# A front without queries and a lag of two slices in a gated mixture-of-experts block on one core

## The reference

```
kv   = ctx @ Wk.T + bk
sim  = ((LN(x) @ kv) @ kv.T) / 16              # 256 x 256 per batch
attn = softmax((sim - mean) * rsqrt(var + 1e-6) * gamma + beta)
x1   = x + tanh(g0) * attn
h    = LN(x1)
score = sigmoid(h @ Wg.T)                      # 16 experts in 4 groups
# with a bias: best two groups by their top two, in them the top 4 experts;
# weights = the scores of those four, normalised, times 2.5
out  = x1 + tanh(g1) * (shared(h) + sum_e weight_e * down_e(silu(gate_e h) * up_e h))
```

## Time and profile before

| | us |
|---|---|
| median of 3 runs | 194.6 (194.2 to 194.71) |
| profiled execution, its time | 194.61 |
| its span in the profile | 192.8 |
| PE busy | 183.1 (95%) |
| DVE busy | 147.1 (76%) |
| ACT busy | 81.2 (42%) |
| POOL busy | 83.0 (43%) |

### The profile page before, as it was taken

The page is one execution under the profiler, slowest core; times in us unless marked ns, Lnnn a source line. Parts: engine busy times, 40 slices in busy tenths (PEclk is TensorE's granted clock), DMA queues, the critical chain, the costliest instruction groups (busy, mean ns, idle before and its releaser), DMA issues.

```text
span 192.8 us, 3265 instructions
## 1 busy us (share of the span) xinstructions
PE 183.1 (95%) x1003; PEld 151.9 (79%) x1003; DVE 147.1 (76%) x332; ACT 81.2 (42%) x160; POOL 83.0 (43%) x101
## 2 busy tenths in 40 slices
PE   6999799969899999999999989999999999999993
PEld 5665457858788888888788868888888888888882
DVE  1759988989899699998469999885666665566664
ACT  2449725523248833435457333434334343433220
POOL 2352162822841755553345543454444555444410
PEclk9999999999999999999999999999999999999999
DMA  5967200002785555541221000312211221221403
GB/s 145 344 212 217 76 0 0 0 0 57 235 205 183 150 141 163 161 139 58 54 54 54 0 3 9 109 57 74 80 60 54 54 54 60 74 78 60 143 20 112
DMA packets 10297, 18.08 MB, mean 94 GB/s; under 512 B 1773, under 2 KB 3821, under 8 KB 10286
## 3 DMA queue, kind: packets, MB, share of 16 engines
q1 hardware_dynamic: 9504, 17.11, 29.4%
q10 hardware_dynamic: 782, 0.83, 1.8%
HBM read 16.82 MB, written 1.11 MB: 93 GB/s over the span
## 4 chain that ended last, share of the span: by engine, by line
PE 67%; DVE 20%; DMA 6%; issue 2%; POOL 1%; ACT 1%; DVEq 0%; SPq 0%; POOLq 0%
PE bank L782 41%; PE bank L834 8%; PE bank L826 7%; PE bank L828 7%; DMA xs<-x_in 3%; DVE act_hi L553 2%; DVE bank L556 2%; DVE act_lo L561 2%; DMA w_row<-weight_rows 2%; DVE stats L458 1%; POOL rstd L278 1%; PE bank L712 1%; DMA weight_rows<-w_blk 1%; DVE beats L597 1%; PE bank L752 1%
## 5 line engine op out<-in xcount | busy, mean ns | idle before, releaser
L284 POOL TENSOR_TENSOR w_lo<-w_raw,w_hi 128x256 fp32r<-128x256 f32 (+1 forms) x72 | 72.4, 1024 | 76.7 <-ACT w_hi L327 75.6
L327 ACT CAST w_hi<-w_raw 128x256 fp32r<-128x256 f32 (+2 forms) x72 | 36.5, 513 | 56.4 <-PE bank L834 30.6
L782 PE MATMUL bank<-hT_hi,w_hi 128*128 128x512 f32 x142 | 56.5, 398 | 0.0
L782 PE MATMUL bank<-hT_lo,w_hi 128*128 128x512 f32 x142 | 56.0, 395 | 0.0
L782 PE MATMUL bank<-hT_hi,w_lo 128*128 128x512 f32 x142 | 44.7, 396 | 0.0
L535 DVE TENSOR_TENSOR weighted<-bank,w_row 128x512 f32<-128x512 f32 x30 | 20.7, 691 | 25.6 <-ACT bank L386 24.5
L826 PE MATMUL bank<-w_hi,act_hi 128*128 128x256 f32 x144 | 36.0, 283 | 1.8 <-DVE act_hi L553 1.8
L828 PE MATMUL bank<-w_lo,act_hi 128*128 128x256 f32 x144 | 35.8, 281 | 0.0
L782 PEld LDWEIGHTS bank<-hT_hi,w_lo 128*128 128x128 f32 x142 | 26.7, 188 | 6.3
L782 PEld LDWEIGHTS bank<-hT_hi,w_hi 128*128 128x128 f32 x142 | 26.8, 189 | 5.1
L826 PEld LDWEIGHTS bank<-w_hi,act_hi 128*128 128x128 f32 x144 | 27.2, 189 | 4.3 <-issue 2.8
(11 more groups left out here) (100 smaller groups left out, 133.2 us busy)
## 6 DMA issues: line engine op xcount, KB each, us to landing
w_row<-weight_rows SPq DMA_DIRECT2D x31, 256.0 KB, 3.2
w_raw<-w_in SPq DMA_DIRECT2D x18, 384.0 KB, 3.9
xs<-x_in SPq DMA_DIRECT2D x4, 256.0 KB, 5.9
out<-x SPq DMA_DIRECT2D x2, 256.0 KB, 3.5
cw<-ctxw_in ACTq DMA_DIRECT2D x1, 276.2 KB
vec<-vecs_in ACTq DMA_DIRECT2D x1, 265.0 KB, 5.6
out<-x SPq DMA_DIRECT2D x2, 128.0 KB, 1.8
out<-x ACTq DMA_DIRECT2D x2, 128.0 KB, 1.8
```

Of the source, the lines that this page charges most:

```text
L284: nc.gpsimd.tensor_tensor(w_lo[:, par, cols], w_raw[:, bass.ds(n, 1), cols].rearrange("p o c -> p (o c)"), w_hi[:, par, cols].bitcast(F32) ...
L327: nc.scalar.copy(w_hi[:, par, cols], w_raw[:, bass.ds(n, 1), cols].rearrange("p o c -> p (o c)"))\
L782: last = nc.tensor.matmul(dst, w[:, par, w0 + c * P:w0 + (c + 1) * P], m, start=i == 0, stop=i == len(parts) - 1, skip_group_check=True)
```

## The change

1. Front without queries. The host passes x transposed too (xT), and the context with a row of ones, as columns (cT) and as rows. PE makes `square` = Wk' Wk from the augmented weights, u = square times the centred context (`projected`), r = context rows times xT (`gathered`), and sim = r u. Centring the context (`centre_context`, DVE for batches 0 and 1, ACT for 2 and 3) takes the mean out of sim. x isn't normalised any more; a term `row_eps` of x's variance goes into the variance of sim instead.
2. Logits of batches 0 and 1. POOL multiplies u with gamma (`u_times_gamma`), PE makes a second product from it (`similarity_gamma`), ACT scales its rows by the inverse root (`scale_rows`), and one DVE operation adds -beta and takes the minimum (L547, `tensor_tensor_reduce`); exp has the scale -1. Batches 2 and 3 keep scale, add and maximum on DVE.
3. The table of exp is loaded early by an activation on two columns; contexts lead the queues of SP and ACT.
4. Lag of two: in step k PE does down of k-2. act_hi, act_lo and the down weights (now d_hi, d_lo) have three buffers. gate(k) still waits for `act_done` of k-2.
5. Gate and up of slices 0 and 1 for batch 0 run on PE before the transposes of batch 1 (`early_gate`, `early_up`), with pieces of batches 2 and 3 between; `route(0)` stands inside step 0 and `route_back(0)` inside step 1.
6. DVE's routing of half 0 stands in one piece after step 1. The late multiplications of slices 2 and 3 by the weight row (`late_parts`) move to step 3 and write to SBUF.
7. All loops are unrolled; the load of a weight row waits for `actlo_done` where it waited for `act_done`.

The core of the diff:

```diff
+            def u_times_gamma(b):
+                pool.wait_ge(u_ready, b + 1)
+                nc.gpsimd.tensor_tensor(uT_gamma[:, b, :], uT[:, b, :], gamma_key[:], ALU.mult)\
+                  .then_inc(u_gamma_ready, 1)
...
+            def scale_rows(b):
+
+                act.wait_ge(rstd_ready, b + 1)
+                for i, t in enumerate(tiles(b)):
+                    act.wait_ge(scaled_done, 2 * b + i + 1)
+                    nc.scalar.activation(scaled[:, t, :], scaled_ps[b][i], ACT.Identity,
+                                         scale=rstd[:, 1, t:t + 1]).then_inc(scaled_read, 1)
...
+            table_change = {7: lambda: (softmax_exp(2), softmax_exp(3)), 16: lambda: logit_exp(1)}
+
+            u_copy(0)
+            r_copy(0)
+            offset_copy(1)
+            r_copy(1)
+            u_copy(1)
+            scale_rows(0)
+            softmax_exp(0)
+            high_gu(0)
...
             hidden_high(1)
+            offset_copy(3)
+            u_copy(3)
             logitT_copy(0)
-            logit_exp(0)
             each_step(act, step, {
-                12: [lambda: hidden_high(2), lambda: hidden_high(3)],
-                13: [lambda: logitT_copy(1)],
+                1: [lambda: logit_exp(0)],
+                13: [lambda: hidden_high(2), lambda: hidden_high(3)],
+                14: [lambda: logitT_copy(1)],
...
+            def sim_logits_negative(b):
+
+                for i, t in enumerate(tiles(b)):
+                    dve.wait_ge(scaled_read, 2 * b + i + 1)
+                    nc.vector.tensor_tensor_reduce(logit[:, t, :], scaled[:, t, :], beta_neg[:], 1.0, BIG, ALU.add, ALU.min,
+                                                   neg_max[:, t:t + 1]).then_inc(max_ready[b], 1)
...
+            def weighted_late(k, par):
+
+                ins = nc.vector.tensor_tensor(weighted[:, par, :], up_ps[par][:, :], weighted[:, par, :], ALU.mult)
+                ins.then_inc(act_done, 1)
+                dve.wait_ge(act_done, k + 1)
+
+            def late_parts(k):
+
+                par, own = k % 2, k % 3
+                if k == NSH:
+                    dve.wait_ge(first_row_done, 1)
+                    row = first_row_ps[:, :]
+                else:
+                    dve.wait_ge(row_in[par], 16)
+                    row = w_row[:, par, :]
+                if k >= 3:
+                    dve.wait_ge(down_done, k - 2)
+                nc.vector.tensor_tensor(act_hi[:, own, :], row, weighted[:, par, :], ALU.mult).then_inc(acthi_done, 1)
+                link(nc.vector.tensor_tensor(weighted[:, par, :], row, weighted[:, par, :], ALU.mult))
+                dve.wait_ge(acthi_done, k + 1)
+                nc.vector.tensor_tensor(act_lo[:, own, :], weighted[:, par, :], act_hi[:, own, :].bitcast(F32),
+                                        ALU.subtract).then_inc(actlo_done, 1)
...
             each_step(dve, step, {
-                0: [rank_groups, mask_groups],
-                1: [lambda: pick_experts(0)],
-                2: [lambda: sim_stats(3), lambda: sim_centre(3)],
-                4: [lambda: sim_logits(2, 9)],
-                5: [lambda: sim_logits(3, 10)],
-                7: [lambda: attention_scale(2), lambda: residual(2)],
-                8: [lambda: x1_stats(2)],
-                9: [lambda: attention_scale(3), lambda: residual(3)],
-                10: [lambda: x1_stats(3)],
-                11: [lambda: normalise(2, 2, 11, x1, hid, hid_ready), lambda: normalise(2, 3, 12, x1, hid, hid_ready)],
-                12: [lambda: hidden_low(2), lambda: hidden_low(3)],
-                14: [lambda: add_logits(1)],
-                15: [lambda: score_groups(1), rank_groups],
-                16: [mask_groups],
-                17: [lambda: pick_experts(1)],
-                NF: [lambda: result(0)],
-                NF + 1: [lambda: result(1)],
+                0: [],
+                1: [lambda: add_logits(0), lambda: score_groups(0), rank_groups, mask_groups, lambda: pick_experts(0)],
+                2: [lambda: sim_stats(2), lambda: sim_scale(2)],
+                3: [lambda: late_parts(2), lambda: x_stats(3), lambda: sim_stats(3), lambda: late_parts(3)],
+                4: [lambda: sim_scale(3)],
+                5: [lambda: sim_logits(2, 5)],
+                6: [lambda: sim_logits(3, 6)],
+                8: [lambda: attention_scale(2), lambda: residual(2)],
+                9: [lambda: x1_stats(2)],
+                10: [lambda: attention_scale(3), lambda: residual(3)],
+                11: [lambda: x1_stats(3)],
+                12: [lambda: normalise(2, 2, 7, x1, hid, hid_ready), lambda: normalise(2, 3, 8, x1, hid, hid_ready)],
+                13: [lambda: hidden_low(2), lambda: hidden_low(3)],
+                15: [lambda: add_logits(1)],
+                16: [lambda: score_groups(1), rank_groups],
+                17: [mask_groups, lambda: pick_experts(1)],
...
+
+                gate_up(k, par, k // NF)
+                if k >= 2:
+                    if k % NF == 2:
+                        pe.wait_ge(score_ready, k // NF + 1)
+                    down(k - 2)
...
-                    product(k, gate_ps[par][:, :], 0, moving, par, midway).then_inc(gate_done, 1)
-                if first >= 2:
-                    pe.wait_ge(actlo_done, k - 1)
+                if k < 2:
+                    early_gate(k, 1).then_inc(gate_done, 1)
+                    if k == 0:
+                        route(0)
+                    else:
+                        route_back(0)
+                    early_up(k, 1).then_inc(up_done, 1)
+                    return
+
...
+            keep_warm(9, bank[0])
             pe.wait_ge(ident_ready, 2)
-            transposes(0, lnT_ps, ln, ln_ready, lnT_done)
-            transposes(1, lnT_ps, ln, ln_ready, lnT_done)
-            keep_warm(2, bank[7])
-            query(0)
-            pe.wait_ge(kv_ready, 1)
-            project(1)
-            similarity(0)
-            query(1)
-            pe.wait_ge(kvT_ready, 2)
-            project_transposed(2)
-            similarity(1)
-            keep_warm(4, bank[7])
-            pe.wait_ge(kvT_ready, 3)
-            project_transposed(3)
-            for b in (2, 3):
-                transposes(b, lnT_ps, ln, ln_ready, lnT_done)
-            for b in (2, 3):
-                query(b)
-            for b in (2, 3):
-                similarity(b)
-            keep_warm(6, bank[5])
+            pe.wait_ge(r_ready, 3)
             hidden(0)
+            keep_warm(2, bank[0])
+            early_gate(0, 0)
+            early_up(0, 0)
+            offset(2)
+            early_gate(1, 0)
+            projected(2)
+            early_up(1, 0)
+            pe.wait_ge(u_ready, 3)
             hidden(1)
-            first_gate(0)
-            route(0)
+            offset(3)
+            similarity(2)
+            projected(3)
             each_step(pe, step, {
-                12: [lambda: hidden(2), lambda: hidden(3)],
-                13: [lambda: route(1)],
-                14: [lambda: route_back(1)],
+                0: [lambda: similarity(3)],
+                13: [lambda: hidden(2), lambda: hidden(3)],
+                14: [lambda: route(1)],
+                15: [lambda: route_back(1)],
```

628 lines of the change are left out of this document (349 added, 279 removed).

## The result

The change made the kernel slower: 204.1 us in the median of 4 runs (201.7 to 205.7) against 194.6 (194.2 to 194.7) for the kernel before on the same chip, a ratio of 1.041 [1.034, 1.048], with the 95% interval in brackets. The traced execution took 203.21, with a span of 201.1, so it is 8.6 us above the one shown of before (194.61, 192.8).

A forecast was written before the change was run, and what follows sets the result against it. PE is full except where VectorE makes it wait: act_hi(0) at 33.2 plus 25.7 puts gate(6) at 58.9; then 131.8 of work, 3.0 of waits, 3.2 of tail and 1.8 around the span give 198.7 us, range 194.5 to 201.5.

The forecast's parts named there:

- What held the kernel, and the direction: Whole kernel: PE is full except where VectorE makes it wait, gate(6) waits for act_done(4); slower by over 0.3%, chance 0.79.
- The front, 22.6 for the first gate: Work ahead of the first gate: without queries it starts at 22.6 us, 5.0 earlier than before.
- the similarity's statistics start at 10.0: DVE in the front: after context, centring, x's statistics and negated beta, these statistics begin at 10.0 us, 3.8 earlier.
- The copy at 30.7, act_hi(0) at 33.2: First routing: 8.1 us of PE work delays the logits' copy, so act_hi(0) gains only 0.5 of 5.0 us.
- Rival E: Table change ahead of the first silu: ScalarE held twice 1.28 us, act_hi(0) at 34.5, time 200.0; chance 0.02.
- The stretch of 25.7 us: VectorE from act_hi(0) to act_done(4): 20.9 before, plus 5.6 of added work, less 0.8, ending at 58.9 us.
- rival B: Routing and late parts on DVE: no pauses beside POOL, saving about 2 us, time 196.6; chance 0.22.
- From gate(6) on: 131.8 and waits of 3.0: From 58.9 us to the last matmul: 131.8 us of PE work plus 3.0 of waits (1 to 4.5).
- 0.8 over the steps that carry batches 2 and 3: Steps after gate(8), ahead of the second routing: PE waits 0.8 us in all, part of the 3.0 of waits.
- A: Gate(4) to gate(6): VectorE's stretch is shorter and lag two swallows it, faster, 189.4 if PE never waits; chance 0.12.
- D: Front and stretch: the front's gain reaches act_hi(0) in part and pauses are few, no difference, 194.6; chance 0.06.
- C: Front not earlier: late contexts or fused operation at 1.0; first gate 24.5 or 25, time 200.5; chance 0.16.

The follow-up runs named there:

- e_hid: Against the changed kernel, transposes of h for batches 2 and 3, second routing and its pieces one step later; 201.2 to 203.3 us, ratio 1.035 to the kernel before.
- the version that repairs the loss: Changed kernel with shorter front, later hidden rows, first silus ahead of similarities and routing, batch 3's x statistics in DVE's gap; rerun 194.2 to 195.9 us, ratio 1.001.

## Why the prediction was wrong

*What held the kernel, and the direction.* Right. Gate(6) waits for DVE's second operation on slice 4, act_hi(0) gains next to nothing (0.5 us was forecast, it came 1.94 later), the front's gain is lost to the copy of the logits, and downs don't wait for act_hi (only 0.2 us for act_lo). The experiments show the chain where the work behind act_hi(0) stays the same: in four traces gate(6) follows 24.28 or 24.29 us behind act_hi(0), at 32.77 to 37.95. It doesn't hold whatever the order: with the early silu the distance is 28.94, and with the filler matmuls 24.94, where PE at the lower clock ends last. PE's waits between 36 us and gate(6) sum to 4.9 us, less than the 7.2 forecast, since PE itself came to slice 2 later than forecast.

*The front, 22.6 for the first gate.* Wrong by 1.6: 24.23. The step that failed is "the similarity's statistics start at 10.0". The context landed at 7.45, inside my bounds of 5.25 to 8.1 but above the 6.4 taken, and DVE then waited 1.22 us for the broadcast vectors that the negated beta reads, a transfer that my sum of the front didn't have at all: 12.08. The fused operations went the other way: the second ended at 15.4, 3.3 us behind the start of the statistics where I had 3.8. From there to the first gate it took 8.8 us, as forecast. So 2.1 - 0.5 = 1.6. (The forecast's own terms give 13.7 for that end, not 13.8.) The vectors aren't all of the 2.1: the product that these statistics read ended on PE at 11.44, so without the vectors they could have begun at about 11.5, an estimate. The sum had VectorE's rows alone and no term for PE's chain up to that product either. In the kernel with the shorter front, where the vectors are out of the way, the statistics wait 1.22 us for it and begin at 10.91, still 0.9 behind the forecast.

*The copy at 30.7, act_hi(0) at 33.2.* Wrong by 2.45: 33.08 and 35.65. Of it, 1.63 is the later first gate; the rest is 8.85 us instead of 8.1 between gate and copy. In the runs with the same order and no low clock there it took 7.90 to 7.94, so the count of matmuls was right and the clock made the difference of 0.9. Silu, load and copy were as counted.

*The table load.* It takes 1.28 us at 33.67 and the silu starts at 34.97, right behind it, as in the earlier trace rows. The Trainium skill, "ScalarE: Activation LUTs", section "What ACT_TABLE_LOAD costs", adds a drain of about 1.38 us to a switch; no row of this case shows one, and the measurement decides. Rival E falls.

*The stretch of 25.7 us.* It was 24.29, 1.4 less, mainly because the routing rows I had expected to be long beside POOL, as the earlier trace rows show them, mostly weren't (0.23 at 42.47; 0.95 at 43.24 was the longest of them): above their usual time they hold 0.7 us, before 1.8. That is rival B's mechanism in part, and the errors cancelled in part: gate(6) was forecast for 58.9 and came at 59.94.

*From gate(6) on: 131.8 and waits of 3.0.* Wrong by 3.25: 138.05 instead of 134.8. The failed term is "0.8 over the steps that carry batches 2 and 3". DVE was busy 39.1 of 41.9 us there, the hidden rows were 1.73 late on PE (1.50 and 0.23), the low clock that followed lost another 1.70, for which the sum had no term at all; the waits for gates after gate(6) were 1.2 in three. These make 4.6 of the 6.25 us above 131.8; 1.6 stand in no wait's row (before, 1.3 of the 2.0 didn't either), and the second routing, where I had 1.0, cost nothing (PE 20.00 of 20.00). That a step's delay doesn't help shows in e_hid, the kernel with the hidden rows a step later: the wait for them goes, and one of 1.97 for the second routing's weight row comes. That the low clock belongs to the wait isn't shown: behind the same waits it fell in three traces (the kernel after, the same kernel again and the shorter front) and not in three others. The pauses beside POOL, which I had put into the first stretch, came mostly in this one: the long rows of DVE between 35 and 98 us hold 6.9 us above their usual time, 5.2 of it behind 60 us; before, it is 2.6, all of it ahead of 52.

*The rest.* The tail was 0.1 shorter than forecast, what lies around the span 0.3 longer. Sum: 2.45 - 1.4 + 3.25 - 0.1 + 0.3 = 4.5, which is 203.2 less 198.7.

*Rivals.* A and D (faster, no difference) needed less work in the stretch than there was or a front that reached act_hi(0). B's shorter stretch happened without B's time. C named a later first gate, 24.5 to 25, and an act_hi(0) 1.7 to 2 later, and gave 200.5; its front was nearly what came, but not by its reasons (the context landed ahead of the late bound and the fused operation was cheaper than taken), and the part behind gate(6) was not. My range had no case for a low clock: the earlier trace rows showed a full one, and I took it as given.

What the change did to the kernel: in this order of work the saving of the front isn't reached, because DVE stood idle for 4.6 us and then had the work of three places in one stretch. With the order of the version that repairs the loss, it is reached at gate(6), 5.4 us earlier than before in the first trace and 4.4 in the second, and mostly used up afterwards: one down owed, 1.4, and from gate(6) on 2.5 us of waits and late rows more than before (136.4 from gate(6) to the end of the last matmul in the first trace, 136.5 in the second, against 132.5 and the 1.4; 1.7 of it is the one gate that waits behind the second routing's weight row), then 0.2 to 0.3 around the span. That leaves 1.3 us in the first trace, 0.2 in the second, and nothing in the ratio of the runs. How much of the loss is the low clock's stays open: the kernel after had one in each of its nine executions, with a mean granted clock of 0.974 to 0.983, and no experiment took it away with all else the same.

## What to carry to other kernels

If one engine is full from a point on, ask two things of a change first: when that engine gets its first piece, and what the sum of its pieces is; reordering them was worth about 1.5 us at gate(6) here, by an estimate. An earlier start is worth something only if all it needs (here both silus, PE's products and the weight row) comes early too, and of work taken out (3.1 us here) only so much comes back (1.2) until another wait ends last. List every transfer that an instruction in the front waits for, those of small constants first, since in a list in order one late vector delays everything behind it. Where a change adds waits of the matrix engine, give the range a case for a low clock (1.7 us each here), though the waits don't tell where it falls. And read a front from several traces: the same one varied by 2.7 us here.

## What the runs showed of the hardware

- TensorE's granted clock fell to 1.2 GHz for about 3.4 us, 1.7 us lost, at 23.3 us and at 98.4 us of the kernel after, each time with two waits of PE shortly before (1.39 and 0.77; 1.50 and 0.23). It did not fall behind 1.78 and 0.95 at 46 to 50 us of the same execution, and did behind 1.78 and 0.76 in the kernel with filler matmuls, there for nearly 7 us. Behind waits of 1.50 or 1.51 and 0.23 or 0.24 for the hidden rows it did not fall with the gap filled, the early silu and routing in the old order. The traced execution of the kernel before had waits of 1.39 and 0.7 us and no low clock; but other executions of it, beside the experiments, had a mean granted clock of 0.987 to 0.991 and took 195.2 us or more, against 194.1 to 195.2 at 0.996 to 1.000. Which wait is followed isn't settled.
- The fused add-and-minimum with its reduction took 0.43 us for 128x256 and an accumulator read of 0.08, and the next began 0.37 behind: cheaper than an add of 0.48 and a maximum of 0.34 apart.
- A row of 2 columns (at 77.99) took 0.92 us and ended with POOL's operation beside it, where its kind takes 0.23 (17.00 to 17.23 in the front). So, by this one row, even the smallest rows with inputs from SBUF can be held for what is left of a POOL operation.
